# Receiver rows as three bfloat16 parts in the products of a graph attention layer

## What is computed

```python
sent  = nodes[senders] @ Ws + Ws_b
e_att = sent + edges @ We + We_b
recv  = nodes[receivers] @ Wr + Wr_b
logits = mish(e_att + recv) . attn_w + attn_b        # per head
w = softmax of logits over the edges of one receiver
out_nodes = segment_sum(w * e_att, receivers)
out = layernorm(x + out_nodes)
```

## Time and profile before

| | |
|---|---|
| median of 3 runs | 3909.14 us (3900.53, 3909.14, 3909.86) |
| profiled execution | 3882.45 us, its span 3880.6 us |
| granted TensorE clock, mean | 0.747 |
| busy PE, PEld, DVE, ACT, POOL | 1900.8, 1818.1, 1878.8, 1681.8, 1552.4 us |
| gathers L694 | x1632, mean 951 ns |
| products of the edges L785 | x3264 recorded (two halves each), 722.5 us, mean 307 ns |
| products of the receivers L786 | x3264 recorded, 705.3 us, mean 302 ns; weight loads 568.9 us, mean 218 ns |
| ACT copies L909, L916 | x408 each, mean 585 and 590 ns |
| longest wait in total | ACT, copy L909, for "remote": 1390.9 us, 70 pieces |

### The profile page before, as it was taken

One profiled execution on the slowest core, in us unless ns is written; L12 is line 12 of the kernel. 1 busy time (PEld: TensorE's weight loads), 2 busy tenths in 40 slices (PEclk: granted clock), 3 DMA queues, 4 the chain that ended last, 5 costly groups with the idle time before them and its releaser, 6 DMA issues.

```text
span 3880.6 us, 49688 instructions
## 1 busy us (share of the span) xinstructions
PE 1900.8 (49%) x15454; PEld 1818.1 (47%) x15454; DVE 1878.8 (48%) x4399; ACT 1681.8 (43%) x2921; POOL 1552.4 (40%) x1640
## 2 busy tenths in 40 slices
PE   3345534544553553454364355356445445435536
PEld 3345534533543553454354355355445445435536
DVE  2435544544543554454465355445445445445537
ACT  0335534533543453453354354345335445435435
POOL 3443353344344334334434434433433543443440
PEclk8777777876876787787677677677668777767868
DMA  6111221211211121121121212212112112111220
GB/s 183 54 57 47 75 61 49 74 58 54 69 58 58 46 76 58 52 72 58 54 71 56 58 51 73 58 49 75 58 52 71 59 56 71 58 56 47 76 59 10
DMA packets 107469, 240.31 MB, mean 62 GB/s; under 512 B 46429, under 2 KB 73300, under 8 KB 100412
## 3 DMA queue, kind: packets, MB, share of 16 engines
q0 software_dynamic: 52224, 107.06, 10.5%
q1 hardware_dynamic: 53074, 132.41, 9.9%
q10 hardware_dynamic: 2142, 0.49, 0.1%
HBM read 230.09 MB, written 9.74 MB: 62 GB/s over the span
## 4 chain that ended last, share of the span: by engine, by line
another core or an unknown queue 32%; PE 26%; issue 21%; DVE 17%; ACT 1%; ACTq 1%; DVEq 1%
PE ps_z L785 7%; PE ps_z L786 6%; PE ps_sum L819 6%; DVE tbuf L1163 3%; DVE tbuf L1142 3%; DVE Z L1124 3%; DVE onehot L1113 2%; PE ps_edgeT L766 2%; DVE tbuf L1135 2%; PE ps_onehotT L771 2%; PE ps_ends L808 2%; PE ps_ends L800 1%; DVE Z L1232 1%; PE ps_ends L827 1%
## 5 line engine op out<-in xcount | busy, mean ns | idle before, releaser
L694 POOL DMA_INDIRECT gath<-xs_table,src_i x1632 | 1551.4, 951 | 2234.7 <-DVE Z L1124 1239.6
L785 PE MATMUL ps_z<-we_sb,edgeT 128*128 128x128 f32 x3264 | 722.5, 307 | 1545.7 <-ACT edgeT L909 888.2
L785 PEld LDWEIGHTS ps_z<-we_sb,edgeT 128*128 128x128 f32 x3264 | 564.8, 217 | 1569.6 <-ACT edgeT L909 904.0
L1124 DVE TENSOR_TENSOR Z<-ps_z,gath 128x512 f32<-128x512 f32 x408 | 280.9, 688 | 1616.5 <-remote 1076.6
L909 ACT COPY edgeT<-ps_edgeT 128x512 f32<-128x512 f32 x408 | 238.7, 585 | 1550.8 <-remote 1390.9
L786 PE MATMUL ps_z<-xr_buf,onehotT 128*128 128x128 f32 x3264 | 705.3, 302 | 0.0
L786 PEld LDWEIGHTS ps_z<-xr_buf,onehotT 128*128 128x128 f32 x3264 | 568.9, 218 | 0.0
L819 PE MATMUL ps_sum<-Z,onehot 128*128 128x132 f32 x3264 | 446.2, 286 | 17.0 <-issue 12.5
L819 PEld LDWEIGHTS ps_sum<-Z,onehot 128*128 128x128 f32 x3264 | 403.3, 195 | 15.3 <-issue 10.6
L940 ACT ACTIVATE ps_ratio<-tbuf,c_ln 128x512 f32<-128x512 f32 x408 | 281.8, 691 | 188.8 <-issue 120.3
L916 ACT CAST onehotT<-ps_onehotT 128x512 f32<-128x512 bf16 x408 | 240.6, 590 | 247.9 <-remote 122.0
(11 more groups left out here) (113 smaller groups left out, 1695.0 us busy)
## 6 DMA issues: line engine op xcount, KB each, us to landing
edge_buf<-in_edge_attr_dram SPq DMA_DIRECT2D x51, 2048.0 KB, 7.9
gath<-xs_table,src_i POOLq DMA_INDIRECT x1632
xr_buf<-xr_table SPq DMA_DIRECT2D x51, 64.0 KB
xr_in<-xr_table SPq DMA_DIRECT2D x51, 64.0 KB
x_in<-in_x_dram SPq DMA_DIRECT2D x51, 64.0 KB
out_dram<-y_out SPq DMA_DIRECT2D x51, 64.0 KB, 1.6
xs_table<-onehot SPq DMA_DIRECT2D x2, 896.0 KB
xr_table<-Z SPq DMA_DIRECT2D x1, 1568.0 KB
```

The lines of the kernel that those rows point to most:

```text
L694: nc.gpsimd.indirect_dma_start(gath[:, b, t, :], None, xs_dram, bass.IndirectOffsetOnAxis(ap=src_i[:, b, t:t + 1], axis=0))\
L785: nc.tensor.matmul(ps_z[q][:, j, :], edgeT[:, q, j, :], we_sb[:, :], start=True, stop=False)
L1124: nc.vector.tensor_tensor(Zv[:, b, a:a + n, 0:D], ps_z[g % 2][:, 0:n, :], gath[:, b, a:a + n, :], ALU.add).then_inc(z_ready, 1)
```

## The change

The receiver rows of a window (128x128 float) are split into three bfloat16 tiles, high, middle and low, whose sum is the float row with its full 24 bits: the first is the row rounded to bfloat16, the second the rounded rest, the third what is left. Four DVE steps in a new function `split_receivers` do it; they are the four parts of `aside` in g7, for the next window, and stand once ahead of the loop for the first. `onehotT` becomes bfloat16 (ones and zeros are exact in it), and PE adds the receivers by three bfloat16 products a tile in place of one float product. The products of g0 now wait for the last of the four steps (`split`) and no longer for the landing of `xr_buf`, for which the first step waits.

```diff
+PARTS = 3
+SPLIT = 4
...
+        xr_parts = sb("xr_parts", [P, 2, PARTS, D], BF16)
+        xr_rest = sb("xr_rest", [P, D])
...
-        onehotT = sb("onehotT", [P, 2, GT, P])
+        onehotT = sb("onehotT", [P, 2, GT, P], BF16)
...
+        split = sem("split")
...
                 if g == 0:
-                    pe.wait_ge(xr_landed[b], k * 16 + 16)
+                    pe.wait_ge(split, w * SPLIT + SPLIT)
                 for j in range(n):
                     nc.tensor.matmul(ps_z[q][:, j, :], edgeT[:, q, j, :], we_sb[:, :], start=True, stop=False)
-                    mm = nc.tensor.matmul(ps_z[q][:, j, :], onehotT[:, q, j, :], xr_buf[:, b, :],
-                                          start=False, stop=True)
+                    for c in range(PARTS):
+                        mm = nc.tensor.matmul(ps_z[q][:, j, :], onehotT[:, q, j, :], xr_parts[:, b, c, :],
+                                              start=False, stop=(c == PARTS - 1))
                 mm.then_inc(z_ps, 1)
...
+            def split_receivers(w, b, k, part):
+
+                base = w * SPLIT
+                high, middle, low = [xr_parts[:, b, c, :] for c in range(PARTS)]
+                if part == 0:
+                    dve.wait_ge(xr_landed[b], k * 16 + 16)
+                    nc.vector.tensor_copy(high, xr_buf[:, b, :]).then_inc(split, 1)
+                elif part == 1:
+                    dve.wait_ge(split, base + 1)
+                    nc.vector.tensor_tensor(xr_rest[:, :], xr_buf[:, b, :], high, ALU.subtract).then_inc(split, 1)
+                elif part == 2:
+                    dve.wait_ge(split, base + 2)
+                    nc.vector.tensor_copy(middle, xr_rest[:, :]).then_inc(split, 1)
+                elif part == 3:
+                    dve.wait_ge(split, base + 3)
+                    nc.vector.tensor_tensor(low, xr_rest[:, :], middle, ALU.subtract).then_inc(split, 1)
...
+                if g == 7 and there(w + 1) and there(w):
+                    split_receivers(w + 1, 1 - b, k + b if b else k, part)
...
             look_for_unsorted()
+            for part in range(SPLIT):
+                split_receivers(0, 0, 0, part)
             run(dve, window)
```

## The result

| | before | after |
|---|---|---|
| median of 4 runs each, us | 3906.6 (3900.5 to 3909.9) | 4047.8 (4039.5 to 4055.2) |
| ratio | 1 | 1.0361, 95% interval 1.0340 to 1.0382 |
| profiled execution, time and span | 3882.5, 3880.6 | 4046.6, 4044.7 |
| mean granted clock | 0.747 | 0.729 |

A forecast was written before the change was run, and what follows sets the result against it. Each window was taken as 40 us of gathers, 6 until g5's release, work bound by PE then DVE up to `normalise`, and a load chain. The sum was 3909.1 - 12.7 + 1.0 + 3 = 3900 us, range 3878 to 3926.

The forecast's parts named there:

- The products: PE, groups g5 to g7: three bfloat16 products replace one float product, so the add of g7 comes 0.68 us earlier.
- marks: Trace signs named beforehand as showing the forecast right or wrong, such as 12.4 us from g5's first product to g7's add.
- Rival 3: On PE, bfloat16 weight loads not overlapping passes set the pace: 3985 us, or 3944 by the skill's 81 ns; chance 0.10.
- The cast: ACT's cast of the one-hots writes half the bytes, but width does not show in its time: 0.
- The split: Two casts and two subtractions on DVE between the steps of g7 delay `normalise` by 0.41 us, bounds 0.12 to 1.0.
- The start: Four dependent split steps before the first window add 1.0 us.
- The new wait: PE's g0 products wait for the last split: add of g0 1.92 us behind `normalise`, not 0.85, off the burst's path.
- the 0.23 that DVE was to get back at g2: DVE waits for PE at g2, so 0.23 of the 1.07 us returns, leaving g3 and g4 0.83 us later.
- What that lateness costs: Later g3 against the burst: 5 of 8 short intervals lost at 4.0 us each, +20 us in an execution like the profiled one.
- rival 2: The hold deepens: PE's completion at g3's end arrives only at burst end, 2.3 us per interval, 4008 us; chance 0.05.
- The argument against it: Against the deeper hold: in the latest windows g3's maxima still come 23 us into the burst, 22 before its release.

The follow-up runs named there:

- e10: The kernel before (float product, no split) with PE holding the products of g0 until DVE's reduction in g7; delayed, 3934.8 us, ratio 1.0159.
- e15: The kernel before with its float product, plus the four split steps in g7 and PE's wait for them; delayed, 4010.2 us, ratio 1.0351.
- e1: The kernel after with the four split steps moved from g7 to g5; undelayed, 2148.9 us, ratio 1.0002.
- e11: The kernel after with the split in g5 and the float product behind the bfloat16 ones in every second tile; delayed, 3898.1 us, ratio 1.0067.
- e3: The kernel after with a group's four float products ahead of its twelve bfloat16 ones; undelayed, 2192.8 us, ratio 1.0196.
- e7: The kernel after with the split in g5 and a group's four float products ahead of its bfloat16 ones; undelayed, 2152.5 us, ratio 1.0023.
- e16: The kernel before with only the added wait of PE for DVE's reduction in g7, run once more; delayed, 3935.4 us, ratio 1.0175.

## Why the prediction was wrong, step by step

*The products, -0.68 us.* The spacing was right (0.056 forecast 0.055), the sum was not. I read it from a row of four bfloat16 passes and left out the float load that follows them, 0.055 us in three tiles of four. The add of g7 follows that of g6 by 4.29, not 4.12; before it is 4.35. So 0.06 per group, some 0.2 in all. One of the marks met its value all the same: from g5's first product to the add of g7 it is 12.1 us in the median window, 12.4 forecast, 13.1 before. That was luck: the products make 0.2 of it, the rest is that g5 begins 3 us later in the burst and the clock is at its upper level more often by then. Rival 3 named the mechanism (loads that passes don't cover) and priced it for the wrong instructions. The Trainium skill's 81 ns (TensorE: Matmul & The Clock Gate, Back-to-back issue gap) is met by no row here: 56 ns within the bfloat16 passes, 111 where a float load is in it. By the page the three groups would have lost 0.25 us, by my row gained 0.68; they gained 0.2.

*The cast*, 0: right. *The split*, +0.41 on DVE: right, 0.42 (`normalise` 4.00 behind the add of g7). *The start*, +1.0: the four steps take 1.2 us, but the burst at 251.04 stands 4.8 us later than in before. The first add of the loop, inside a burst, comes at 137.1 us and not at 125.0, so the delay was there already.

*The new wait, add of g0 1.92 behind `normalise`.* Measured 2.17 at full clock, because I gave the products 1.5 us from the first to the last and they take 1.77 (three float loads behind bfloat16 passes, and a first product slower behind idle time); and 2.8 to 3.7 in 21 windows, in which the clock is at its lower level during the products, as it never is in before. I had listed who waits for the new wait, not what PE's idleness does to PE. And of the 0.23 that DVE was to get back at g2 it got 0.07 in the median window. Instead of 0.83 us, g2 is 1.93 us later against the burst.

*What that lateness costs: the step that failed.* I let it cost only the short intervals, 5 lost at 4.0 us each, +20 us, and put the long ones at nothing. And I put the number of matmuls that PE issues in a burst at nothing, though each group has four more. Together the two put the add of g5 3.3 us later in the burst on average, 154 us in all 47 intervals. Lateness is the greater part: with the wait and the float product alone the loss is 62 us (e10), with the split steps 138 (e15); but at the same lateness after has the add of g5 2.4 us later than e15. Of 46 intervals in before, 8 have the add of g5 at 45 to 47 us and 38 at 49 to 50; in after none and 18 (up to 50.9), and 15 have it at 51 to 53 and 13 at 54 to 55. That is nearest to rival 2, the deeper hold, at a chance of 0.05, and its 2.3 us per interval were too few. The argument against it, that the latest windows of before still got their maxima 23 us in, looked at windows with g3 0.8 us later than the mean (5.7 us in, not 4.9), and the shift was 1.93. The slope could have been looked for: over before and after together the interval is 72.6 us with the add of g2 on average 1.8 ahead of the burst (10 intervals), 75.0 at 1.0 ahead (36), 76.3 at its start (22), 77.7 at 0.9 inside (15), 79.7 at 2.1 (9), some 1.6 us per us. All but one of the intervals in the first two of these groups are of before. A smaller slip: the intervals with g3 at most 4.45 us in are 10, not 11 (in the first, the add 2.4 us in is g1's), and moved by 0.83 none stays early. It changes the +20 by some 2 us.

*Of the marks that I named*, long intervals near 74.9 and g3 added 5.5 us into the burst were to show the forecast right; they are 77.5 (77.75 with the first) and 22. "Wrong" was to show as a release later than 46 us. The release itself hardly moved: results come through in a crowd at some 45 us as before, but they are those of g3, not of g4, in the worst windows.

## What to carry to other kernels

A wait that moves work off the critical path in one place moves it against something else: find out what the moved work runs into next and what it costs per microsecond there, over all windows and not only the odd ones. A new wait on PE costs its length and the clock that the idle time takes, and three short products gain only what the wider weight loads around them leave. Here the same split two groups earlier takes the loss away undelayed (e1) and, together with an alternating order of the products, all but 26 us of it delayed (e11).

## What the runs showed of the hardware

- One program, one set of inputs, two conditions: 2149 and 3872 us, by whether PE's results reach the other engines while POOL issues gathers. One chip had both at different times.
- Delayed, results reach DVE the later, the more matmuls PE has issued since the burst's start (medians: the 40th to 47th 12 us in, the 56th to 63rd 37, later ones 45). At equal lateness the kernel with more matmuls is held longer (g5 at 52.8 and 50.4 us, after and e15).
- A float weight load behind a bfloat16 pass costs 0.055 us at full clock. A group of four tiles, three bfloat16 products in each, takes 1.73 us with three such places (after), 1.67 with two (e11), 1.56 with none (e3, e7).
- The granted clock during the products of g0 was at its lower level in none of 47 windows without idle time of PE ahead of them (before), in 10 after 1.2 to 1.3 us (e16), and after 1.6 us in 33 with float products (e15) and 21 with bfloat16 ones (after).
